# One GpSimd wait for two blocks' gather buffers in the edge loop of a graph network layer

## Chip, cores and metric

The kernel runs on one core of a Trainium2 chip (trn2). The metric is device time in microseconds; lower is better. Five engines run side by side and wait for one another through semaphores: PE (TensorE, matmuls), DVE (VectorE), ACT (ScalarE), POOL (GpSimd) and SP (SyncE, which here only issues DMAs).

## What is computed

One message-passing layer on 6250 nodes of 128 features and 100000 edges. Each edge gathers the rows of its two end nodes, a three-layer network makes a message, messages are averaged by destination, and a second network updates the node; a residual and a layer normalisation close it. Edges come sorted by destination (`col`).

```python
row, col = (edge_index[0], edge_index[1])
msg_in = jnp.concatenate([node_features[row], node_features[col]], axis=-1)
h = jax.nn.relu(msg_in @ Wm1 + bm1)
h = jax.nn.relu(h @ Wm2 + bm2)
messages = h @ Wm3 + bm3
agg = jax.ops.segment_sum(messages, col, num_segments=num_nodes)
...
agg = agg / jnp.clip(count, 1.0)[:, None]
node_in = jnp.concatenate([node_features, agg], axis=-1)
upd = jax.nn.relu(node_in @ Wn1 + bn1) @ Wn2 + bn2
return node_features + upd
```

## The kernel before

There are three stages. **Preparation** computes per node the two halves of the first product, x @ Wm1[:128] + bm1 and x @ Wm1[128:], and stores them in HBM as `a_table` (256 f32 a node) and `b_table`. **The edge loop** takes the edges in 391 blocks of 256 (EB; two halves of 128, TB = 2). **The node update** works on 49 windows of 128 nodes.

In the loop a block b goes through these steps, each on its engine and in that engine's program order; buffers rotate by the block's number:

- GpSimd (line 624) issues two indirect DMAs, one for each half: 128 rows of `a_table`, chosen by `src_idx`, into one of R = 4 buffer pairs of `a_edge`. Their landing counts on `s_g[b % 4]`. From the fifth block on it waits ahead of them (lines 621 and 622 of the source before) until PE has transposed block b - 4, whose buffers it fills: `s_ta` counts one for each block transposed.
- SP (lines 531 to 542) loads `rel` for two blocks at every even block, and, block by block, waits for both gathers of b (`s_g`, line 540) and issues the load of `b_win` (line 541), a window of 128 rows of `b_table`, into one of RB = 4 buffers. Once in four blocks it also reads the addresses of the next four windows from memory.
- DVE makes `onehot_t` of b (line 1013) when `b_win` of b has landed. In its program this stands two steps ahead: after the low part `h` (line 1104) of block b - 2.
- PE waits for `onehot_t` of b (`s_ot`), and this one wait covers the gathers too, since the `b_win` load was issued after their landing. It transposes the four 128x128 pieces of `a_edge` into PSUM (line 1365, four matmuls, the last counts on `s_ta`) and adds `b_win` x `onehot_t` (line 1311). Then it sums the messages of block b - 5 (lines 1328 to 1336, four matmuls) and does the second product of block b - 2 (line 1407, twelve matmuls), for which it waits for DVE's `h`.
- ACT takes relu of the first product (line 731), which DVE splits into a high and a low float32r part (line 1104), and likewise the second product (lines 721 and 1098). DVE also makes `onehot` (line 1028) and adds finished sums into `agg` (line 1050).

On SP, PE, ACT and DVE the blocks run in bodies of U = 4 in a hardware loop. GpSimd's loop over the blocks is unrolled: 387 waits and 782 gathers in a row, and no other work until the loop's end.

Of the kernel before, what the change touches and what calls it, by code (L numbers as in the profile page):

```python
# [19 lines left out]
R = 4  # L20
# [13 lines left out]
def gnn_layer(nc, x, src, dst, Wm1, bm1, Wm2, bm2, Wm3, bm3, Wn1, bn1, Wn2, bn2, out):  # L34
# [6 lines left out]
    NBE = -(-E // EB)  # L41
# [18 lines left out]
    with ExitStack() as ctx:  # L60
# [3 lines left out]
        def sem(name):  # L64
            return ctx.enter_context(nc.semaphore(name))
# [197 lines left out]
        s_ta = sem("s_a_transposed")  # L263
# [97 lines left out]
        def b_uses(k, g):  # L361

            return sum(b_at(j) == k for j in range(g))
# [202 lines left out]
        @block.gpsimd  # L566
        def _(pool):
            pool.memset(ident[:, :], 0.0).then_inc(s_zeros, 1)
            pool.wait_ge(s_zeros, 1)
            pool.affine_select(out=ident[:, :], in_=ident[:, :], compare_op=ALU.not_equal, fill=1.0,  # L570
                               base=0, pattern=[[-1, P]], channel_multiplier=1).then_inc(s_const, 1)
            pool.memset(edges_in[:, (GR - 1) * EB:GR * EB], PAD_DST).then_inc(s_pad, 1)
            pool.memset(edges_in[:, (2 * GR - 1) * EB:2 * GR * EB], 0).then_inc(s_pad, 1)
            pool.memset(f_x[:, NW - 1, :], 0.0).then_inc(s_xz, 1)
            pool.memset(ones2[:, :].bitcast(F32), 0.0).then_inc(s_zeros, 1)
            for rows in (b3_rows, bn2_rows):
                pool.memset(rows[:, :].bitcast(F32), 0.0).then_inc(s_zeros, 1)
            pool.wait_ge(s_zeros, 4)
            pool.memset(ones2[0:2, :].bitcast(F32), 1.0).then_inc(s_const, 1)
            pool.memset(h2_hi[:, :, :, H:HC].bitcast(F32), 1.0).then_inc(s_const, 1)  # L580
            pool.iota(node_half_i[:, :], pattern=[[P, NFE + 1]], base=0, channel_multiplier=1,
                      allow_small_or_imprecise_dtypes=True).then_inc(s_const, 1)
            pool.iota(first_node[:, :], pattern=[[P, NW]], base=0, channel_multiplier=0,
                      allow_small_or_imprecise_dtypes=True).then_inc(s_const, 1)
            pool.iota(iota16[:, :, :], pattern=[[0, TB], [1, P]], base=0, channel_multiplier=0,
                      allow_small_or_imprecise_dtypes=True).then_inc(s_const, 1)
            pool.memset(zeros[:, :], 0.0).then_inc(s_const, 1)
            pool.memset(from_quarter[:, :], 1.0).then_inc(s_mask, 1)
            pool.memset(to_quarter[:, :], 1.0).then_inc(s_mask, 1)
            pool.wait_ge(s_mask, 2)  # L590
            pool.affine_select(out=from_quarter[:, :], in_=from_quarter[:, :], compare_op=ALU.is_ge, fill=0.0,
                               base=0, pattern=[[-QUARTER, P // QUARTER]], channel_multiplier=1).then_inc(s_mask, 1)
            pool.affine_select(out=to_quarter[:, :], in_=to_quarter[:, :], compare_op=ALU.is_ge, fill=0.0,
                               base=-1, pattern=[[QUARTER, P // QUARTER]], channel_multiplier=-1).then_inc(s_mask, 1)
            pool.memset(words_act[0:1, :], 0).then_inc(s_wz, 1)
            pool.memset(words_pe[0:1, :], 0).then_inc(s_wz, 1)
            pool.memset(words_dve[0:1, :], 0).then_inc(s_wz, 1)
            pool.memset(row_step[0:1, :], 2).then_inc(s_wz, 1)
            pool.memset(row_far[0:1, :], 0).then_inc(s_const, 1)

            pool.wait_ge(s_edges, 16 * len(loads))
            pool.tensor_copy(edges_f[0:BG, GR:2 * GR, :],
                             edges_in[0:BG, GR * EB:2 * GR * EB].rearrange("p (g e) -> p g e", g=GR)
                             ).then_inc(s_efs, 1)
            dst_f = edges_f[0:BG, 0:GR, :]
            pool.tensor_copy(dst_f, edges_in[0:BG, 0:GR * EB].rearrange("p (g e) -> p g e", g=GR)).then_inc(s_efd, 1)

            pool.wait_ge(s_et, 2 * GR)
            pool.wait_ge(s_scr_rel, 16 * GR)
            pool.wait_ge(s_bz, 16)  # L610
            pool.wait_ge(s_w2s, 1)
            pool.wait_ge(s_fl, 1)
            pool.wait_ge(s_rw, 11)
            pool.memset(agg[:, :], 0.0).then_inc(s_zero, 1)

            for k in range(2):
                pool.wait_ge(s_as[k], 16 * ((NG + 1 - k) // 2))
            pool.wait_ge(s_bs[2], 16 * b_uses(2, NG))
            pool.wait_ge(s_ec, GR)
            for b in range(NBE):  # L620
                if b >= R:
                    pool.wait_ge(s_ta, b - R + 1)
                for t in range(TB):
                    pool.indirect_dma_start(a_edge[:, b % R * TB + t, :], None, a_table,  # L624
                                            bass.IndirectOffsetOnAxis(ap=src_idx[:, b * TB + t:b * TB + t + 1],
                                                                      axis=0)
                                            ).then_inc(s_g[b % R], 16)
            pool.wait_ge(s_w2, NBE)
            for k in range(2):
                pool.memset(f_row[k].bitcast(F32), 0.0).then_inc(s_frz, 1)  # L630
# [843 lines left out]
```

## Time and profile before

| | us |
|---|---|
| median of 3 timed runs | 1221.72 |
| the three runs | 1220.55, 1221.72, 1224.82 |
| span of the profiled execution | 1422.7 |
| edge loop in it, 89 to 1325 us | 1236 |
| PE busy / DVE / ACT / POOL in it, whole span | 1256.0 / 969.2 / 728.3 / 772.3 |

The profiled execution is a run of its own, and here it is 201 us longer than the timed median; recording weighs on this kernel. Times of records are true within it, and a timed run is shorter. PE's clock is granted in full (0.99 on average). A matmul's recorded end is modelled, and two neighbours overlap, so spacings of starts are read rather than lengths. A release that the profile can't name stands as "remote", and "issue" is idle time in which an engine waited for nothing that is shown.

### The profile page before, as it was taken

The page shows a single profiled execution, that of the slowest core. Times are in us where ns is not written, and L with a number is a line of the kernel's source. Part 1 is how long each engine was busy: PE and PEld are TensorE (multiplying, and loading weights), DVE is VectorE, ACT ScalarE, POOL GpSimd, SP SyncE. Part 2 cuts the span into 40 slices and gives each one's busy share as a digit, 9 for nine tenths or more (in the row PEclk, how much of TensorE's full clock was granted, in tenths as well). Part 3 has the DMA queues.
Part 4 walks back from the last instruction along what each step waited for, and adds up shares of the span by engine and source line. Part 5 has one row for each costly group of instructions (what it writes and reads, how often), then busy time and mean ns, then how long its engine had stood idle before and what let it go on. Part 6 is the DMA issues. An engine that isn't in the chain of part 4 may idle for free.

```text
span 1422.7 us, 34295 instructions
## 1 busy us (share of the span) xinstructions
PE 1256.0 (88%) x9586; PEld 1169.5 (82%) x9587; DVE 969.2 (68%) x2072; ACT 728.3 (51%) x1392; POOL 772.3 (54%) x814
## 2 busy tenths in 40 slices
PE   6978988888889988998889888999888988899897
PEld 5868888888888888888888888888888888888786
DVE  6856666666666666666666766767676776777676
ACT  3544554554554554554555454545545445455585
POOL 2166666666666665666666656666656666664000
PEclk9999999999999999999999999999999999999999
DMA  9765555455444545555445545454554445555012
GB/s 303 284 222 153 144 146 147 146 146 148 144 147 143 149 147 146 145 145 147 147 144 146 149 144 146 143 150 142 145 147 144 144 144 147 147 143 151 15 65 87
DMA packets 135603, 211.39 MB, mean 149 GB/s; under 512 B 24247, under 2 KB 102669, under 8 KB 134030
## 3 DMA queue, kind: packets, MB, share of 16 engines
q1 hardware_dynamic: 98030, 108.43, 25.5%
q0 software_dynamic: 37536, 102.55, 24.7%
q8 instruction: 13, 0.21, 0.1%
q14 instruction: 24, 0.20, 0.0%
HBM read 188.09 MB, written 22.80 MB: 148 GB/s over the span
## 4 chain that ended last, share of the span: by engine, by line
PE 58%; issue 16%; DVE 6%; another core or an unknown queue 6%; ACT 5%; DVEq 4%; DMA 2%; POOL 1%; SPq 1%; ACTq 0%
PE bank L1407 27%; PE bank L1365 9%; PE bank L1311 5%; PE sums L1328 4%; ACT bank L728 2%; PE sums L1332 2%; PE bank L1438 2%; PE sums L1336 2%; PE sums L1334 2%; ACT h L731 2%; PE sums L1451 1%; DVE h_lo L1098 1%; DVE onehot_t L1013 1%; DVE h L1104 1%
## 5 line engine op out<-in xcount | busy, mean ns | idle before, releaser
L624 POOL DMA_INDIRECT a_edge<-a_table,src_idx x782 | 752.9, 963 | 479.8 <-remote 280.5
L1407 PE MATMUL bank<-w,h 128*128 128x256 f32 x4692 | 655.4, 283 | 93.7 <-issue 92.6
L1407 PEld LDWEIGHTS bank<-w,h 128*128 128x128 f32 x4692 | 595.6, 189 | 116.7 <-issue 116.2
L721 ACT ACTIVATE h_hi<-bank 128x512 fp32r<-128x512 f32 x391 | 234.6, 600 | 453.3 <-remote 360.6
L1098 DVE SCALAR_TENSOR_TENSOR h_lo<-bank,h_hi 128x512 fp32r<-128x512 f32 x391 | 267.6, 685 | 137.5 <-issue 132.5
L1104 DVE SCALAR_TENSOR_TENSOR h<-bank,h 128x512 fp32r<-128x512 f32 x391 | 268.3, 686 | 105.9 <-ACT h L731 53.5
L731 ACT ACTIVATE h<-bank 128x512 fp32r<-128x512 f32 x391 | 234.1, 599 | 135.5 <-remote 62.2
L1365 PE MATMUL bank<-ident,a_edge 128*128 128x128 f32 x1564 | 241.8, 277 | 35.7 <-DVE onehot_t L1013 18.8
L1028 DVE SCALAR_TENSOR_TENSOR onehot<-iota,first_node,dst_col 128x256 fp32r<-128x256 int16 x391 | 187.4, 479 | 88.0 <-issue 86.5
L728 ACT COPY bank<-b_bc 128x512 f32<-128x512 f32 x391 | 234.8, 600 | 23.5 <-DVE h_lo L1098 17.4
L1365 PEld LDWEIGHTS bank<-ident,a_edge 128*128 128x128 f32 x1564 | 177.8, 141 | 54.2 <-DVE onehot_t L1013 30.7
L1311 PE MATMUL bank<-onehot_t,b_win 128*128 128x256 f32 x782 | 189.7, 324 | 0.9 <-issue 0.8
L1013 DVE TENSOR_SCALAR onehot_t<-rel,node_half 128x256 fp32r<-128x256 int16 x391 | 137.8, 352 | 11.9 <-DMA b_win<-b_table 9.3
L1328 PE MATMUL sums<-h_hi,onehot 128*128 128x258 f32 x391 | 125.3, 321 | 4.2 <-DVE h_lo L1098 1.0
L1311 PEld LDWEIGHTS bank<-onehot_t,b_win 128*128 128x128 f32 x782 | 119.1, 192 | 1.8 <-issue 1.6
L1332 PE MATMUL sums<-h_lo,onehot 128*128 128x256 f32 x391 | 114.5, 293 | 0.1
L1334 PE MATMUL sums<-h_hi,onehot 128*128 128x258 f32 x391 | 110.8, 283 | 0.0
L1336 PE MATMUL sums<-h_lo,onehot 128*128 128x256 f32 x391 | 109.7, 281 | 0.0
L1328 PEld LDWEIGHTS sums<-h_hi,onehot 128*128 128x128 f32 x391 | 73.4, 188 | 26.2 <-issue 22.2
L1332 PEld LDWEIGHTS sums<-h_lo,onehot 128*128 128x128 f32 x391 | 73.7, 188 | 5.3 <-issue 4.7
L1334 PEld LDWEIGHTS sums<-h_hi,onehot 128*128 128x128 f32 x391 | 74.5, 190 | 0.0
L1336 PEld LDWEIGHTS sums<-h_lo,onehot 128*128 128x128 f32 x391 | 73.7, 188 | 0.0
(186 smaller groups left out, 668.5 us busy)
## 6 DMA issues: line engine op xcount, KB each, us to landing
b_win<-b_table SPq DMA_DIRECT2D x391, 128.0 KB
rel<-rel_dram SPq DMA_DIRECT2D x196, 128.0 KB
a_edge<-a_table,src_idx POOLq DMA_INDIRECT x782
a_table<-work SPq DMA_DIRECT2D x12, 512.0 KB, 4.8
b_table<-work SPq DMA_DIRECT2D x5, 1024.0 KB
b_table<-h SPq DMA_DIRECT2D x4, 1024.0 KB
f_x<-in_x SPq DMA_DIRECT2D x12, 256.0 KB, 6.0
b_table<-a_edge SPq DMA_DIRECT2D x3, 1024.0 KB, 6.1
```

The lines of the kernel that those rows point to most:

```text
L624: pool.indirect_dma_start(a_edge[:, b % R * TB + t, :], None, a_table, bass.IndirectOffsetOnAxis(ap=src_idx[:, b * TB + t:b * TB + t + 1], ...
L721: act.activation(h2_hi[:, (k - AHEAD - 1) % U, :, 0:H], bank[H2[(k - AHEAD - 1) % U]][:, :].rearrange("p (t h) -> p t h", t=TB), ACT.Relu) ...
L728: act.copy(bank[H2[k % U]][:, :], b2_bc[:, :, :].rearrange("p t h -> p (t h)"))
L731: act.activation(h1[:, k % U, 0, :], bank[k % 2][:, :], ACT.Relu).then_inc(s_h1h, 1)
L1098: dve.scalar_tensor_tensor(h2_lo[:, j, :, :], bank[H2[j]][:, :].rearrange("p (t h) -> p t h", t=TB), 0.0, h2_hi[:, j, :, 0:H].bitcast(F32) ...
L1104: dve.scalar_tensor_tensor(h1[:, k % U, 1, :], bank[k % 2][:, :], 0.0, h1[:, k % U, 0, :].bitcast(F32), ALU.max, ALU.subtract).then_inc(s_ ...
L1311: ins = pe.matmul(bank[k % 2][:, h * EB:(h + 1) * EB], rows[:, h * P:(h + 1) * P], hot, start=False, stop=True, skip_group_check=True)
L1328: return pe.matmul(to[:, 0:HC], onehot[:, slot, 0, :], h2_hi[:, k % U, 0, :], start=start, stop=False, skip_group_check=True)
L1332: pe.matmul(to[:, 0:H], onehot[:, slot, 0, :], h2_lo[:, k % U, 0, :], start=False, stop=False, skip_group_check=True)
L1334: pe.matmul(to[:, 0:HC], onehot[:, slot, 1, :], h2_hi[:, k % U, 1, :], start=False, stop=False, skip_group_check=True)
L1365: ins = pe.matmul(bank[k % 2][:, h * EB + t * P:h * EB + (t + 1) * P], a_edge[:, k % R * TB + t, h * P:(h + 1) * P], ident[:, :], start=(t ...
L1407: ins = pe.matmul(to, h1[:, j, a, h * EB + t * P:h * EB + (t + 1) * P], w2[:, b, h, :], start=False, stop=(a == 1 and h == KH - 1), skip_g ...
```

## The change

```diff
@@ -618,8 +618,8 @@
             pool.wait_ge(s_ec, GR)
             for b in range(NBE):
-                if b >= R:
-                    pool.wait_ge(s_ta, b - R + 1)
+                if b >= R and b % 2 == 0:
+                    pool.wait_ge(s_ta, min(b - R + 2, NBE))
                 for t in range(TB):
                     pool.indirect_dma_start(a_edge[:, b % R * TB + t, :], None, a_table,
```

GpSimd waits at even blocks only, for both blocks whose buffers it fills next: ahead of the gathers of b and b + 1 it waits until b - 3 is transposed, where it waited for b - 4 ahead of b and for b - 3 ahead of b + 1. Four gathers follow each wait. Nothing else is altered; the buffers, the other engines' programs and the amount of work are the same.

GpSimd's instructions at the start of the edge loop, before. `a_edge` is the gather buffer, `a_table` the table in HBM, `s_a_transposed` the count of transposed blocks; the first eight gathers are those of blocks 0 to 3.

```order
L624 DMA a_edge<-a_table,src_idx 128x256 [waits s_b_stored2,s_edge_columns,s_a_stored1,s_a_stored0]
L624 DMA a_edge<-a_table,src_idx 128x256 x7
L624 DMA a_edge<-a_table,src_idx 128x256 [waits s_a_transposed]
L624 DMA a_edge<-a_table,src_idx 128x256
L624 DMA a_edge<-a_table,src_idx 128x256 [waits s_a_transposed]
L624 DMA a_edge<-a_table,src_idx 128x256
```

The same place on GpSimd with the change:

```order
L624 DMA a_edge<-a_table,src_idx 128x256 [waits s_b_stored2,s_edge_columns,s_a_stored1,s_a_stored0]
L624 DMA a_edge<-a_table,src_idx 128x256 x7
L624 DMA a_edge<-a_table,src_idx 128x256 [waits s_a_transposed]
L624 DMA a_edge<-a_table,src_idx 128x256 x3
L624 DMA a_edge<-a_table,src_idx 128x256 [waits s_a_transposed]
L624 DMA a_edge<-a_table,src_idx 128x256 x3
```

A wait now stands ahead of every fourth gather instead of every second; the gathers keep their order, and 194 waits remain of 387.

## Rows read from the trace of the kernel before

**Rows 1.** Busy time by stretch: start:end, length, each engine's busy us (instructions).
```profile
core 0: us, PE busy (x) PEld busy (x) DVE busy (x) ACT busy (x) POOL busy (x), PEclk, DMA share, GB/s
0.00:89.00 89.00, 67.19 (x446) 60.24 (x447) 63.60 (x115) 41.93 (x79) 24.59 (x37) 0.98 0.83 294
89.00:1325.00 1236.00, 1105.19 (x8601) 1036.06 (x8602) 839.98 (x1691) 624.24 (x1172) 747.70 (x778) 0.99 0.51 145
1325.00:1422.00 97.00, 83.64 (x541) 73.20 (x539) 65.64 (x266) 62.16 (x141) 0.00 (x0) 0.96 0.18 59
```

**Rows 2.** Costliest groups of the whole span: busy us, mean ns, idle before.
```profile
L624 POOL DMA_INDIRECT a_edge<-a_table,src_idx x782 | 752.9, 963 | 479.8 <-remote 280.5
L1407 PE MATMUL bank<-w,h 128*128 128x256 f32 x4692 | 655.4, 283 | 93.7 <-issue 92.6
...
L1013 DVE TENSOR_SCALAR onehot_t<-rel,node_half 128x256 fp32r<-128x256 int16 x391 | 137.8, 352 | 11.9 <-DMA b_win<-b_table 9.3
```

**Rows 3.** Chain of work that ended last: start us, length, what.
```profile
607.15 0.44 PE bank L1365 x4
...
609.73 0.44 PE bank L1365 x4
```

**Rows 4.** Instructions in time, 700 to 715 us: start, length, engine, line [idle before].
```profile
702.43 0.94 POOL L624 DMA_INDIRECT a_edge<-a_table,src_idx  x1 [0.30 <-issue]
...
703.62 0.34 DVE L1013 TENSOR_SCALAR onehot_t<-rel,node_half 128x256 fp32r<-128x256 int16 x1
...
704.02 0.65 PE L1365 MATMUL bank<-ident,a_edge 128*128 128x128 f32 x4
...
705.40 4.21 SPq L541 DMA_DIRECT2D b_win<-b_table  x2
...
707.55 0.94 POOL L624 DMA_INDIRECT a_edge<-a_table,src_idx  x1 [1.06 <-remote]
...
708.27 0.59 ACT L731 ACTIVATE h<-bank 128x512 fp32r<-128x512 f32 x1
...
708.80 0.95 POOL L624 DMA_INDIRECT a_edge<-a_table,src_idx  x1 [0.30 <-issue]
708.90 0.69 DVE L1104 SCALAR_TENSOR_TENSOR h<-bank,h 128x512 fp32r<-128x512 f32 x1 [0.32 <-ACT h L731]
...
709.50 0.36 DVE L1013 TENSOR_SCALAR onehot_t<-rel,node_half 128x256 fp32r<-128x256 int16 x1
...
709.92 0.66 PE L1365 MATMUL bank<-ident,a_edge 128*128 128x128 f32 x4 [0.19 <-DVE onehot_t L1013]
```

**Rows 5.** The same view at the loop's start; ACT L731 waits for PE L1311.
```profile
89.68 0.78 PE L1311 MATMUL bank<-onehot_t,b_win 128*128 128x256 f32 x2
...
90.49 0.60 ACT L731 ACTIVATE h<-bank 128x512 fp32r<-128x512 f32 x1 [2.56 <-issue]
...
93.23 0.78 PE L1311 MATMUL bank<-onehot_t,b_win 128*128 128x256 f32 x2
...
98.30 0.60 ACT L731 ACTIVATE h<-bank 128x512 fp32r<-128x512 f32 x1 [4.00 <-PE bank L1311]
```

**Rows 6.** The same view in three windows: DVE held by a late b_win load.
```profile
307.24 0.19 SPq L541 DMA_DIRECT2D b_win<-b_table  x1
...
309.87 0.35 DVE L1013 TENSOR_SCALAR onehot_t<-rel,node_half 128x256 fp32r<-128x256 int16 x1 [0.79 <-DMA b_win<-b_table]
...
774.27 1.17 POOL L624 DMA_INDIRECT a_edge<-a_table,src_idx  x1 [0.30 <-issue]
...
778.84 0.25 SPq L541 DMA_DIRECT2D b_win<-b_table  x1
...
781.53 0.35 DVE L1013 TENSOR_SCALAR onehot_t<-rel,node_half 128x256 fp32r<-128x256 int16 x1 [0.47 <-DMA b_win<-b_table]
```

**Rows 7.** Waits of the whole span: total us, times, longest.
```profile
DVE onehot_t L1013 <- DMA b_win<-b_table: 9.3, 18, 2.7
...
SPq L540 <- DMA a_edge<-a_table,src_idx: 166.7, 72, 3.6
```

## Prediction

> **What bounds the kernel now.** I read the table of stretches first: the edge loop takes 1236 us of the 1422.7 us span, 89 us of preparation stand ahead of it and 97 us of node update behind it, and PE is the busiest engine in the loop [rows 1]. The change touches only the loop, so only that stretch is worked out. The loop has 391 blocks (391 `onehot_t`, 782 gathers) [rows 2], so a block takes 1236 / 391 = 3.16 us in the profiled execution. The three timed runs have a median of 1221.72 us, 201 us below the profiled span. If the two ends keep their 186 us, the loop of a timed run is 1036 us, or **2.65 us a block**. In the chain of work that ended last, two neighbouring blocks of nothing but PE work begin their transposes at 607.15 and 609.73 us: 2.58 us apart [rows 3]. 391 x 2.58 is 1009 us, 97% of the timed loop: without the profiler PE is all but the whole bound, and it waits for hardly anything. The extra 0.5 us a block of the profiled execution is idle time called "issue" inside the matmuls of one line (92.6 us on PE) and on the other engines [rows 2].
>
> What releases PE? The transposes of block b wait for `onehot_t` of b (DVE), that one waits for the landing of `b_win` of b, SP issues this load only when both gathers of b have landed, and GpSimd issues the gathers only when the transposes of b - 4 have freed the buffers. So the gathers lie in a ring: **transposes, two gathers, b_win load, onehot_t, transposes**, four blocks round. The change lengthens this ring, and the question is whether it fits into PE's time.
>
> **The ring, link by link.** (a) Transposes to gathers. In the middle of the loop the transposes at 704.02 us are those of block 196 and the gather at 707.55 us is the first of block 200, freed by them: 3.53 us, although the transposes' records end at 704.67 and GpSimd had been idle for 1.06 us [rows 4]. ACT shows the same at the loop's start: at block 0 the activation starts at 90.49, 0.03 us after the recorded end of its matmuls (89.68 + 0.78); at block 2 these matmuls start at 93.23 and the activation at 98.30, after 4.00 us idle waiting for them [rows 5]. The distance is short at first and grows to a whole block within two blocks. I take most of it for the profiler's own burden on PE (it goes with the 201 us) and put 0.9 us for a timed run (0.65 for the transposes, and a reaction between 0.03 and a few tenths); 3.53 us stays as the upper bound. (b) Gather to gather is 1.25 us (707.55 to 708.80) [rows 4]. (c) Second gather to the `b_win` load: 702.43 to 705.40 is 2.97 us [rows 4], and 774.27 to 778.84 is 4.57 us [rows 6], where SP came late for other reasons. SP waited 72 times for a gather, 166.7 us in all [rows 7], so the landing often decides here; I take 3.4. (d) `b_win` load to `onehot_t`, where DVE waited for it: 778.84 to 781.53 is 2.69 us, 307.24 to 309.87 is 2.63 us [rows 6]; I take 2.65. (e) `onehot_t` to transposes: 703.62 to 704.02, 0.40 us [rows 4].
>
> Before: 0.9 + 1.25 + 3.4 + 2.65 + 0.4 = 8.6 us in four blocks, for which PE needs 4 x 2.65 = 10.6 us. There are 2.0 us to spare. In the profile DVE waited only 9.3 us in all for `b_win`, 18 times [rows 7], which agrees.
>
> **The change part by part.** It removes 193 of the 387 waits of GpSimd. Each wait costs GpSimd at most the 0.3 us of idle time that stands ahead of any gather anyway (707.55 + 0.94 to 708.80), and GpSimd is not at the end of the chain, so this gains nothing directly.
>
> What is left moves. *Even blocks*: the wait now asks for the transposes of b - 3, not b - 4. The gathers of b start one block later, and the ring of 8.6 us must close in three blocks, 3 x 2.65 = 7.95 us. It is 0.65 us too long. *Odd blocks*: the gathers of b + 1 wait for the same transposes as before, but now stand behind the two gathers of b that used to have gone ahead: 2 x 1.25 = 2.5 us more, a ring of 11.1 us in four blocks, for which PE needs 10.6. It is 0.5 us too long. Queued behind the one wait on GpSimd are thus four gathers; SP's `b_win` and `rel` loads, in order, wait for their landing, then DVE, then PE. Together: from an odd block's transposes, the even block three later starts at 8.6 us, the odd one behind it at the later of 11.1 and 8.6 + 2.58 = 11.2 us. Four blocks take 11.2 us, 2.80 a block, +0.15 on 2.65. **391 x 0.15 = 58 us, 1222 + 58 = 1280 us.** In the profiled execution, with link (a) at 3.53, the even ring is 11.2 us and four blocks take 11.2 + 2.58 = 13.8 us, 3.45 a block against 3.16: +113 us, a span near 1536 us.
>
> Bounds: with (c) at 2.97 the rings are 8.2 and 10.7 us and a block takes 2.69: +16 us. With (c) at 4.57 always they are 9.8 and 12.3, a block takes 3.09: +172 us. Link (a) can't be 3.53 us in a timed run: in the profile the way from the transposes of block 196 (704.02) over the activation (708.27), DVE's `h` (708.90) and `onehot_t` (709.50) to the transposes of block 198 (709.92) takes 5.90 us [rows 4], and a timed run does two blocks in 5.30, so at least 0.6 us of it is not there. With (a) at 2.9 a block takes (10.6 + 2.58) / 4 = 3.30: +254 us, the upper bound. Below nothing the change can only go by the rival named "faster".
>
> This link is the place where the Trainium skill bears on the case. The row shows 3.53 us from the transposes' start to the gather. The page "TensorE: Matmul & The Clock Gate", section "The cost: per-tile semaphore tail", gives the time from the last matmul's completion to its count as 25 ns plus a few ns a tile and 26 ns a count, under 0.1 us here; the page "Perfetto Trace Analysis", section "Per-instruction lifecycle: what the profiler-reported window actually captures", says that a matmul's end in the profile is estimated and its count comes outside the recorded window. By the first page link (a) would be about 0.75 us, an estimate, and the sum +43 us; by the row it would be the +254 us above. The trace's first block (0.03 us) agrees with the page, its third does not.
>
> **The rivals.** *It fits after all* (not slower): the links are shorter without the profiler. With (c) at 2.7 and (d) at 2.3 the rings are 7.55 and 10.05 us, below 7.95 and 10.6, and PE never waits: 1222 us, within 4 us. It decides from 7.95 us for the even ring on. For it: DVE is rarely held by `b_win` today [rows 7]. Against: today's slack of 2.0 us is what the change spends, 2.65 on even blocks and 2.5 on odd ones. *PE's counts are late in timed runs too*: with (a) between 1.6 and 2.9 us, (a + 7.7 + 2.58) / 4 is 2.97 to 3.30 a block, +125 to +254 us, 1347 to 1476 us. For it: the consumers really start that late, records or not [rows 4, 5]. Against: the timed run is 201 us shorter. *Faster*: with four gathers close together, the transfers of a pair overlap and SP issues two `b_win` loads with less between them, so that GpSimd's 2.5 us in each 2.65 us block lies in fewer, longer pieces and fewer of today's 27 us of leftover stalls (1036 - 1009) remain. It decides only if the rings fit; it could give back 5 to 15 us, 1210 us. Little speaks for it, since the leftover does not stand at gathers. *The change does not do what it says*: the order of instructions shows a wait ahead of every fourth gather, so I give this nothing. GpSimd itself as the limit also needs a look: four gathers take 5.0 us of the 5.3 us of two blocks, it is 6% from being one, and this makes every late wait hard to regain; at 1.33 us a gather it would be the bound.
>
> **How the numbers follow.** A loss of 4 to 125 us, forecast 1280 us: 0.50. Late counts, 1347 us and more: 0.24. It fits, within 0.3% (about what a measurement of this kernel can tell from no change): 0.20. Faster by more: 0.06. The range must leave out no more than 2 in 10: from 1220 us, which keeps the rival that it fits, to 1390 us, which takes in part of the late counts. Faster 0.06, same 0.20, slower 0.50 + 0.24 = 0.74.
>
> **What would show it.** After: GpSimd's gathers in groups of four, 1.25 us apart, with one idle time ahead of each group; more and longer waits of `onehot_t` for `b_win` (today 9.3 us in all; I expect over 60 us), and of the transposes for `onehot_t`; SP's waits for gathers well over today's 166.7 us; blocks in pairs, not evenly spaced; PE's busy time as before; preparation and node update unchanged at 89 and 97 us. Wrong would be the forecast if DVE's wait for `b_win` stays near 9 us, if the odd and even blocks are held alike, or if the profiled span grows much while the timed one does not: then link (a) is the profiler's, and the rest of the ring is shorter than I read it.

## The result and the profile after

| | before | changed |
|---|---|---|
| first comparison, median us | 1221.74 | 1364.47 |
| second, chip 15 (g1) | 1221.18 | 1368.1 |
| third, chip 13 (i1) | 1220.0 | 1362.93 |

The changed kernel is **11.7% slower** (ratio 1.117, 95% interval 1.113 to 1.121; 1.118 and 1.116 in the other two): 143 us, where 58 were forecast. The time lies in the stated range, near its upper end; the direction was right and the size wrong by a factor of nearly 2.5. Each ratio is of undisturbed runs, and one of g4's four runs further down, at 2866.2 us, is left out of it (the other three have a median of 1207.56 us).

One thing must be said of the times first. The kernel before has a median of 1220 to 1224 us on some chips (11, 13, 15 and the one of the first comparison, whose number is not on record) and of 1402 to 1404 us on two others (1 and 3), where no single run is below 1401 us. The profile ahead of the prediction, with its span of 1422.7 us, looks like the second kind: it has the same pauses and the same late counts. So its 201 us over the timed median are not the burden of recording, as was said ahead of the prediction: profiled and timed runs agree on either kind of chip (1223.9 us span in run j1, 1400.2 in run e0). What follows compares kernels on one chip, and j1 stands for the kernel before.

The stretches of the changed kernel, columns as in [rows 1], and then those of the kernel before in run j1 (PEld are PE's weight loads):

```profile
0.00:89.00 89.00, 66.81 (x452) 59.98 (x454) 63.62 (x116) 41.94 (x79) 25.88 (x38) 0.99 0.83 298
89.00:1265.00 1176.00, 1088.08 (x8598) 1021.67 (x8596) 833.53 (x1695) 649.51 (x1172) 747.09 (x777) 1.00 0.54 152
1265.00:1360.00 95.00, 83.34 (x538) 73.08 (x538) 64.24 (x262) 62.18 (x141) 0.00 (x0) 0.95 0.18 60
```

```profile
89.00:1129.00 1040.00, 1025.93 (x8607) 1012.84 (x8608) 825.71 (x1703) 643.06 (x1175) 758.03 (x779) 1.00 0.61 173
1129.00:1224.00 95.00, 83.82 (x534) 73.41 (x532) 62.82 (x256) 61.07 (x139) 0.00 (x0) 0.93 0.18 60
```

Preparation and node update are what they were, 89 and 95 us. The loop went from 1040 to 1176 us, and the weight loads of PE (second pair of numbers) do the same work in it, 1013 and 1022 us: PE waits. The waits name what for. The changed kernel, in total us, times, longest:

```profile
POOL a_edge L624 <- PE bank L1365: 233.2, 193, 3.3
DVE onehot_t L1013 <- DMA b_win<-b_table: 208.5, 182, 3.3
...
PEld bank L1365 <- DVE onehot_t L1013: 109.8, 138, 4.5
...
PEld sums L1328 <- issue: 37.2, 154, 1.2
```

The kernel before, run j1:

```profile
POOL a_edge L624 <- PE bank L1365: 120.3, 316, 2.2
...
DVE onehot_t L1013 <- DMA b_win<-b_table: 76.3, 114, 2.6
...
PEld bank L1365 <- DVE onehot_t L1013: 16.0, 19, 4.2
...
PEld sums L1328 <- issue: 8.2, 35, 1.2
```

GpSimd now waits 193 times, about once in two blocks. DVE waits 182 times for `b_win`, 133 times and 184 of the 208.5 us at even blocks (of which 194 are late), and in all 132 us more than before. PE's weight loads wait 94 us more for `onehot_t` and, a line that the forecast had not looked at, 29 us more for nothing that the profile shows ahead of the sums (L1328). These two make 123 of the loop's 136 us.

The ring can be followed in the trace of the changed kernel from 600 to 613 us: start, length, engine and line, and what ended the idle time before. SPq are the loads that SP issues.

```profile
600.54 0.60 PE L1365 MATMUL bank<-ident,a_edge 128*128 128x128 f32 x4
...
600.77 1.90 SPq L541 DMA_DIRECT2D b_win<-b_table  x2
...
601.41 0.94 POOL L624 DMA_INDIRECT a_edge<-a_table,src_idx  x1 [1.12 <-PE bank L1365]
...
602.66 0.94 POOL L624 DMA_INDIRECT a_edge<-a_table,src_idx  x1 [0.30 <-issue]
...
603.62 0.33 SPq L534 DMA_DIRECT2D rel<-rel_dram  x1
...
603.91 0.95 POOL L624 DMA_INDIRECT a_edge<-a_table,src_idx  x1 [0.30 <-issue]
...
605.16 0.95 POOL L624 DMA_INDIRECT a_edge<-a_table,src_idx  x1 [0.30 <-issue]
...
606.68 2.01 SPq L541 DMA_DIRECT2D b_win<-b_table  x2
...
608.97 0.47 DVE L1013 TENSOR_SCALAR onehot_t<-rel,node_half 128x256 fp32r<-128x256 int16 x1 [0.53 <-DMA b_win<-b_table]
...
609.50 0.66 PE L1365 MATMUL bank<-ident,a_edge 128*128 128x128 f32 x4 [0.51 <-DVE onehot_t L1013]
```

The transposes of odd block 173 (600.54) free GpSimd at 601.41, the second gather of block 176 starts at 602.66, SP loads its `b_win` at 606.68, DVE, which has been waiting, makes `onehot_t` at 608.97, and PE, which has been waiting too, transposes block 176 at 609.50: 0.87 + 1.25 + 4.02 + 2.29 + 0.53 = 8.96 us for three blocks. Averaged over the 183 even blocks from 20 to 384 the same five links are 0.89, 1.27, 3.62, 2.64 and 0.64 us, **9.05 us**. From an even block's transposes to the odd block's behind it there are 2.91 us. 9.05 + 2.91 = 11.96 us in four blocks is the 2.99 us a block of the whole loop. These are averages over all even blocks, not only those where every link was waited for: PE's weight loads waited for `onehot_t` 138 times, and where PE came later than `onehot_t` for another reason, link five is longer than the 0.4 us of a plain reaction.

### The profile page after: what moved, and what is told of

Same layout as the page of the kernel before. It is cut to its first block, busy times and chain, and to the rows that moved or that the text cites. A ratio compares the mean times of both kernels' runs of the same rounds, so it can differ in the third digit from the quotient of the medians.

```text
span 1359.8 us, 34295 instructions
## 1 busy us (share of the span) xinstructions
PE 1238.2 (91%) x9586; PEld 1154.7 (85%) x9587; DVE 961.4 (71%) x2072; ACT 753.6 (55%) x1392; POOL 773.0 (57%) x814
## 4 chain that ended last, share of the span: by engine, by line
DMA 36%; PE 34%; issue 10%; POOL 8%; DVE 6%; DVEq 4%; SPq 2%; ACT 0%
DMA a_edge<-a_table,src_idx 21%; DMA b_win<-b_table 14%; PE bank L1407 10%; POOL a_edge L624 8%; PE bank L1365 7%; DVE onehot_t L1013 3%; PE bank L1438 2%; PE sums L1328 2%; PE bank L1311 2%; PE sums L1451 1%; PE sums L1332 1%; PE bank L1221 1%; PE sums L1334 1%; PE bank L1423 1%; PE sums L1336 1%
## 5 line engine op out<-in xcount | busy, mean ns | idle before, releaser
L1407 PE MATMUL bank<-w,h 128*128 128x256 f32 x4692 | 618.0, 281 | 0.0
L1407 PEld LDWEIGHTS bank<-w,h 128*128 128x128 f32 x4692 | 582.0, 188 | 0.0
L728 ACT COPY bank<-b_bc 128x512 f32<-128x512 f32 x391 | 231.5, 592 | 252.3 <-DVE h_lo L1098 248.9
L1365 PE MATMUL bank<-ident,a_edge 128*128 128x128 f32 x1564 | 244.1, 279 | 81.9 <-DVE onehot_t L1013 80.9
L1013 DVE TENSOR_SCALAR onehot_t<-rel,node_half 128x256 fp32r<-128x256 int16 x391 | 143.2, 366 | 211.0 <-DMA b_win<-b_table 208.5
L1365 PEld LDWEIGHTS bank<-ident,a_edge 128*128 128x128 f32 x1564 | 174.2, 141 | 111.5 <-DVE onehot_t L1013 109.8
L731 ACT ACTIVATE h<-bank 128x512 fp32r<-128x512 f32 x391 | 232.4, 594 | 3.3 <-PE bank L1311 3.3
L1311 PE MATMUL bank<-onehot_t,b_win 128*128 128x256 f32 x782 | 189.0, 323 | 0.0
L1328 PE MATMUL sums<-h_hi,onehot 128*128 128x258 f32 x391 | 129.0, 330 | 7.3 <-DVE h_lo L1098 1.0
L1311 PEld LDWEIGHTS bank<-onehot_t,b_win 128*128 128x128 f32 x782 | 118.6, 192 | 0.2
L1334 PE MATMUL sums<-h_hi,onehot 128*128 128x258 f32 x391 | 110.3, 282 | 0.0
L1328 PEld LDWEIGHTS sums<-h_hi,onehot 128*128 128x128 f32 x391 | 73.2, 187 | 39.4 <-issue 37.2
```

The lines of the kernel that those rows point to most:

```text
L728: act.copy(bank[H2[k % U]][:, :], b2_bc[:, :, :].rearrange("p t h -> p (t h)"))
L731: act.activation(h1[:, k % U, 0, :], bank[k % 2][:, :], ACT.Relu).then_inc(s_h1h, 1)
L1311: ins = pe.matmul(bank[k % 2][:, h * EB:(h + 1) * EB], rows[:, h * P:(h + 1) * P], hot, start=False, stop=True, skip_group_check=True)
L1328: return pe.matmul(to[:, 0:HC], onehot[:, slot, 0, :], h2_hi[:, k % U, 0, :], start=start, stop=False, skip_group_check=True)
L1334: pe.matmul(to[:, 0:HC], onehot[:, slot, 1, :], h2_hi[:, k % U, 1, :], start=False, stop=False, skip_group_check=True)
L1365: ins = pe.matmul(bank[k % 2][:, h * EB + t * P:h * EB + (t + 1) * P], a_edge[:, k % R * TB + t, h * P:(h + 1) * P], ident[:, :], start=(t ...
```

## The experiments

All kernels below compute the full result.

**What sets the 2.99 us: the ring, the queueing, or a price for each late block.** Three kernels keep two gathers to a wait and move only which blocks wait for b - 3 instead of b - 4.

```diff
 # i2, every block
-                    pool.wait_ge(s_ta, b - R + 1)
+                    pool.wait_ge(s_ta, min(b - R + 2, NBE))
 # i3, one block in four (i4: b % 8)
-                    pool.wait_ge(s_ta, b - R + 1)
+                    pool.wait_ge(s_ta, b - R + (2 if b % 4 == 0 else 1))
```

> The changed kernel beside the kernel before and the three placements of the late wait, on one chip. Where the kernel before takes 1222 us: 1361 to 1373 us, as twice before. Where the kernel before takes about 1404 us: the ring bounds the changed kernel there too, and all blocks late took 1418 us there, so 1390 to 1430 us, within 2% of the kernel before, since there the late counts already cost what the ring costs here.

> Every block waits for b - 3 ahead of its own two gathers. Where the kernel before takes 1222 us: ring theory 1355 to 1375 us, queue theory 1222 us, count theory (0.73 us a late block) about 1500 us. Where it takes about 1404: 1418 us as twice before, and ring theory puts it within 20 us of the changed kernel.

> Only every fourth block waits for b - 3. Where the kernel before takes 1222 us: ring theory, 9.05 us and one PE step of 2.6 to 2.9 us in four blocks, 1325 to 1360 us; count theory 1293 us; queue theory 1222 us. Where it takes about 1404: 1471 us as twice before.

> Only every eighth block waits for b - 3. Where the kernel before takes 1222 us: ring theory, 9.05 us and five PE steps of 2.65 to 2.75 us in eight blocks, 1277 to 1300 us; count theory 1258 us; queue theory 1222 us. Where it takes about 1404: 1429 to 1434 us as twice before.

| on one chip, before 1220.0 us | late blocks | median us | ratio (95%) |
|---|---|---|---|
| changed kernel (i1) | 194 | 1362.93 | 1.116 (1.113 to 1.120) |
| all late (i2) | 387 | 1366.92 | 1.123 (1.118 to 1.128) |
| one in four (i3) | 97 | 1366.12 | 1.120 (1.117 to 1.123) |
| one in eight (i4) | 48 | 1309.65 | 1.073 (1.070 to 1.076) |

In i2 every block waits for its own release, and the loss is the same 147 us, so **the loss does not need an odd block queued behind an even one**. The run i3 can't say this: the gathers of block 4j + 1 ask for the same count as those of 4j, so they pass together, and in its trace they follow 1.28 us behind, one after another, as in the changed kernel. But i3 and i4 do rule out a price for each late block, since a quarter, a half or all of the blocks late cost the same 143 to 147 us, and an eighth costs 90. A ring of three blocks once in four sets the pace of all four. In the trace of i3 the way from the transposes of block 4j + 1 to those of 4j + 4 takes 8.88 us and the next step 3.12 us, 12.00 in four blocks; in i2 any three blocks take 9.0; in i4 the ring takes 8.70 us and the five steps behind it 3.22, 2.95, 2.72, 2.63 and 2.69, together 22.91 in eight, 2.86 a block. Two of the three missed what ring theory gave them: i3 lies 6 us above 1325 to 1360 us, i4 10 us above 1277 to 1300. The steps right behind the late block were put too low: 2.6 to 2.9 us in i3, where they take 3.12, and 2.65 to 2.75 in i4, where the first two take 3.22 and 2.95. The waits of i2 and then of i3 are nearly those of the change, with twice and half the late blocks:

```profile
DVE onehot_t L1013 <- DMA b_win<-b_table: 190.2, 182, 2.9
...
PEld bank L1365 <- DVE onehot_t L1013: 110.7, 130, 4.3
```

```profile
DVE onehot_t L1013 <- DMA b_win<-b_table: 224.8, 159, 4.4
...
PEld bank L1365 <- DVE onehot_t L1013: 113.4, 136, 4.8
```

**The same three on chips where the kernel before takes 1402 to 1404 us.**

> Every block waits for b - 3 instead of b - 4 ahead of its own two gathers; there are 387 waits and never four gathers behind one wait. Ring theory: each block is a three-block ring of about 9.05 us (0.89 + 1.27 + 3.62 + 2.64 + 0.64 in the changed kernel's trace), 3.0 a block, so about 1360 to 1370 us, as slow as the change. Queue theory (the loss comes from the odd block's gathers standing behind the even block's): 1222 us. Count theory (each late block costs 0.73 us, 143 us over 195): 387 late blocks, about 1500 us.

> Only every fourth block (b % 4 == 0) waits for b - 3; the others wait for b - 4 as in the kernel before. Ring theory: the slowest loop goes from block 4j + 1 over the ring of 9.05 us to block 4j + 4 and with one PE step of 2.6 to 2.9 us to 4j + 5: 11.65 to 11.95 in four blocks, 2.91 to 2.99 a block, 1325 to 1360 us, nearly the whole loss from half the late blocks. Count theory: 98 late blocks at 0.73 us, 1222 + 71 = 1293 us. Queue theory: 1222 us.

> Only every eighth block waits for b - 3. Ring theory: 9.05 us for three blocks and five PE steps of 2.65 to 2.75 us, 22.3 to 22.8 us in eight, 2.79 to 2.85 a block, 1277 to 1300 us. Count theory: 49 late blocks at 0.73 us, 1258 us. Queue theory: 1222 us.

They took 1418.73, 1472.95 and 1429.27 us beside 1404.05, and on a second such chip (h2, h3, h4) 1417.67, 1470.25 and 1434.41 beside 1402.48. Ring theory's numbers held in none of them, nor did the rivals'. That one late block in four is slower there (4.8 to 5.1%) than all late (1.0%) goes with one difference in the traces. The kernel before and the kernels with one late block in four or eight have, in these runs, 125 to 149 places inside the matmuls of L1407 where the next one starts over 0.3 us later, 91 to 101 us more than the usual spacing in all. With all blocks late (e1 and h2) there is none, and a released gather starts 1.3 us after the transposes. Why PE runs without these pauses when every block is late stays open. The changed kernel fell on no such chip, so what it does there wasn't measured.

**The pairs shifted by one.** The wait stands at odd blocks, for b and b + 1.

```diff
-                if b >= R and b % 2 == 0:
-                    pool.wait_ge(s_ta, min(b - R + 2, NBE))
+                if b == R or b > R and b % 2 == 1:
+                    pool.wait_ge(s_ta, min(b - R + (2 if b > R else 1), NBE))
```

> The changed kernel once more, beside the kernel before on the same chip. On the chip of the runs e0 to e3 the kernel before takes 1404 us, where it took 1222 us in the first comparison. If the change bounds the loop by its ring (9.05 and 2.9 us, 11.95 in four blocks), it does so on any chip: 1355 to 1375 us, faster than a kernel before of 1404 us and slower than one of 1222. If the difference of the chips adds to every kernel alike, it takes 1364 + 182, about 1546 us, there.

> The change with the pairs shifted by one: the wait stands at odd blocks, for b and b + 1, so that the late block is odd and the queued one even. Ring theory: as the changed kernel on the same chip, within 10 us. If SP's own work at even blocks (the rel load, and the addresses once in four blocks) is part of the ring, 10 to 30 us less than the changed kernel.

1356.55 us (ratio 1.111, 1.108 to 1.114) against 1368.1 us for the change on the same chip: 11.5 us less, at the lower edge of what was expected if SP's work at even blocks takes part. The records say where. From the second gather's start to its last data packet the late block takes about 3.15 us on average in g1 and 2.82 us in g2 (to the last landing count 3.5 and 3.2), and the whole ring 9.05 and 8.85. SP's `rel` load, issued at even blocks (at 603.62 us, between the `b_win` loads of 600.77 and 606.68 in the rows of the changed kernel), shares the DMA engines with an even block's gathers and not so much with an odd one's. It is an overlap that fits the numbers; it was not tested by itself.

**The `b_win` load out of the ring.** SP no longer waits for the gathers; DVE does, right ahead of `onehot_t`. The load of `b_win` then starts as soon as SP finds its buffer free, beside the gathers or ahead of them. At even blocks SP waits for that until PE has used `b_win` of b - 3 (it loads `rel` for two blocks there), and in g4 the load starts 1.55 us after the transposes of b - 3.

```diff
-                        if not isinstance(i, int) or i > 0:
-                            sp.wait_ge(s_g[k % R], nth(i, k, 16 * TB))
                         sp.dma_start(b_win[:, k % RB, :].bitcast(F32),
...
-                if isinstance(i, int) and U * i + k < U:
-                    dve.wait_ge(s_g[k % R], nth(i, k, 16 * TB))
+                dve.wait_ge(s_g[k % R], nth(i, k, 16 * TB))
```

It was made in the kernel before (g3), in the changed kernel (g4) and in "all late" (j2).

> The kernel before, with the wait for a block's gathers taken from SP, ahead of the b_win load, to DVE, ahead of onehot_t, so that the b_win load no longer lies in the ring. Ring theory: the ring has slack in the kernel before, so within 0.3% of it where it takes 1222 us. Where it takes 1404 us, the same unless the late counts of PE have used that slack up; then 10 to 60 us less.

> The changed kernel with the same move of the wait to DVE. Ring theory: the even ring is 0.9 + 1.25 + 2.9 (landing of the second gather) + 0.4 + 0.4 = 5.9 us in three blocks, for which PE takes 7.95, and the odd one 8.4 in 10.6: the change's whole loss goes and the time is that of the kernel before with the same move, within 5 us. Rival, four gathers in a row hold GpSimd or the DMA engines too long: it stays slower than that by 20 us or more. Rival, SP's loads are late and not the gathers: as the changed kernel.

> Every block waits for b - 3 (as in all_late), and the wait for the gathers stands on DVE, ahead of onehot_t, so that the b_win load is out of the ring. Ring theory: 0.9 + 1.25 + 2.9 + 0.4 + 0.4 = 5.9 us in three blocks against 7.9 for PE: 1200 to 1212 us, as g3 and g4. If holding a buffer pair one block longer costs by itself, 1300 us or more.

| | median us | before, same chip | ratio (95%) |
|---|---|---|---|
| before with the move (g3) | 1204.36 | 1221.18 | 0.985 (0.982 to 0.988) |
| changed with the move (g4) | 1208.35 | 1221.18 | 0.989 (0.986 to 0.992) |
| all late with the move (j2) | 1208.92 | 1223.66 | 0.987 (0.985 to 0.989) |

The whole loss goes, 1368 to 1208 us, with the single wait and the four gathers in a row still in place. So four gathers in a row cost by themselves at most the 4 us between g3 and g4, whose intervals overlap, and so do the buffers held a block longer (j2); the loss needs the serial load behind them. In g4 DVE waits for the gathers where it waited for `b_win`, and for less than half as long (in g3, g4 and j2 the lines of DVE and PE stand four higher, L1009 for L1013 and L1361 for L1365):

```profile
DVE onehot_t L1009 <- DMA a_edge<-a_table,src_idx: 78.9, 108, 1.8
...
PEld bank L1361 <- DVE onehot_t L1009: 7.9, 6, 4.8
```

g3 came out better than expected (within 0.3% of the kernel before): **it beats both kernels**, by 1.5% over the one before. So the kernel before was already losing some 17 us to this ring. Its 76.3 us of waiting for `b_win` in run j1 fit that, and in g3 that wait is 36.0 us:

```profile
DVE onehot_t L1009 <- DMA b_win<-b_table: 36.0, 81, 2.8
```

**The kernel before, profiled again.**

> The kernel before once more, for a second profile of it. If the late counts of PE in the first profile (3.2 us from the transposes of a block to the gather that they free, against 0.9 us in the profile of the changed kernel) belong to the recording of that one execution, a new profile shows about 0.9 us, a span near 1222 us, and blocks 2.65 us apart. If they belong to this kernel's execution, it shows 3.2 us again, with a span far from the timed 1222 us.

> The kernel before, for a profile on a chip where it takes 1222 us: blocks 2.65 us apart, gathers 0.9 us after the transposes' start where GpSimd waited for them, no pauses inside the matmuls of L1407, DVE waiting for b_win 20 to 60 us in all. Where it takes about 1404 us it repeats the first profile.

e0 (1402.0 us, span 1400.2) and h1 (1404.94 us) repeat the first profile but for its 20 us longer span: from a block's transposes to the gather that they free 3.07 us on average in e0, and pauses inside the twelve matmuls of L1407 (starts over 0.3 us apart), 143 of them, some 94 us in all. j1 (1225.63 us, span 1223.9) has none of these pauses, 0.92 us from transposes to gather, and blocks 2.63 us apart. DVE's wait for `b_win` was expected at 20 to 60 us and is 76.3. Two neighbouring blocks of j1, with the gather that the first one frees:

```profile
605.64 0.60 PE L1365 MATMUL bank<-ident,a_edge 128*128 128x128 f32 x4
...
606.76 0.98 POOL L624 DMA_INDIRECT a_edge<-a_table,src_idx  x1 [0.30 <-issue]
...
608.22 0.60 PE L1365 MATMUL bank<-ident,a_edge 128*128 128x128 f32 x4
```

In [rows 4] such a gather came 3.53 us behind the transposes. Here it is 1.12 us, and GpSimd was still busy with the gather ahead of it: 781.5 us busy in the span and, with 0.30 us between gathers, close to full in the loop.

## Why the prediction was right and wrong

- **What bounds the kernel, 2.65 us a block, 2.58 for PE alone.** Right: run j1 has 2.63 us a block and 89 + 1040 + 95 us, against the 1036 us of loop worked out from the timed median.
- **Link (a), 0.9 us instead of the trace's 3.53.** The value was right (0.92 before, 0.89 changed), and with it the choice against the rival "late counts". The reason given was wrong: the late counts and the 201 us do not come with being profiled. They come with the chip: the same kernel takes 1402 to 1406 us on two of them in all its timed runs, and 1224 with a profile on another. By that, the forecast of a profiled span near 1536 us failed; it was 1359.8.
- **The even ring as the cause.** Right, and shown by g4, where the loss goes with the `b_win` load out of the ring, and by i2, where it stays without the queue.
- **The odd ring, 11.1 us in four blocks.** It does not bind on average. In the changed kernel the last count of the odd block's `b_win` comes 0.70 us ahead of `onehot_t`, that of the even block's 0.24 us, and DVE waits for it 49 times, 25 us in all, at odd blocks. Taking 2.5 us of queueing for a second cause was harmless to the sum, since the even ring and the step behind it already came out longer.
- **The sum, 11.2 us in four blocks.** This is the step that failed: 11.96 were measured. Two terms of it are undersized. The ring is 9.05 us and not 8.6: link (c) 3.62 for 3.4, link (e) 0.64 for 0.40, the rest right to 0.02. And **the PE step behind the late block is 2.91 us and not 2.58**. (0.45 + 0.33) / 4 x 391 is 76 us; with 8 us because the kernel before has 2.63 and not 2.65 us a block, 58 becomes 142, the loss measured.
- **Why that step is longer.** 2.58 us was read where PE had just been busy [rows 3]. Behind a late block PE itself is slower; DVE, in order, also comes late, but seldom later than PE. In the trace of the changed kernel, a block that PE had not waited for, and then block 176, the late one:

```profile
606.26 0.60 PE L1365 MATMUL bank<-ident,a_edge 128*128 128x128 f32 x4
...
606.93 0.28 PE L1328 MATMUL sums<-h_hi,onehot 128*128 128x258 f32 x1
...
607.41 1.58 PE L1407 MATMUL bank<-w,h 128*128 128x256 f32 x12
```

```profile
609.59 0.48 DVE L1050 SCALAR_TENSOR_TENSOR agg<-sums,to_quarter,agg  x1
...
610.47 0.48 DVE L1028 SCALAR_TENSOR_TENSOR onehot<-iota,first_node,dst_col 128x256 fp32r<-128x256 int16 x1 [0.39 <-issue]
610.47 0.19 PEld L1328 LDWEIGHTS sums<-h_hi,onehot 128*128 128x128 f32 x1 [0.29 <-issue]
...
611.05 1.58 PE L1407 MATMUL bank<-w,h 128*128 128x256 f32 x12
...
611.47 0.68 DVE L1104 SCALAR_TENSOR_TENSOR h<-bank,h 128x512 fp32r<-128x512 f32 x1
612.07 0.34 DVE L1013 TENSOR_SCALAR onehot_t<-rel,node_half 128x256 fp32r<-128x256 int16 x1
...
612.47 0.66 PE L1365 MATMUL bank<-ident,a_edge 128*128 128x128 f32 x4
```

  From the transposes to the twelve matmuls of L1407 there are 1.15 us in the first (606.26 to 607.41) and 1.55 us in the second (609.50 to 611.05), with 0.29 us of "issue" ahead of the sums. It is so on average: between blocks 20 and 380 of the changed kernel this way takes 1.53 us in the 124 blocks for which PE had waited, and 1.15 us in g3, where it never waits. The twelve matmuls take the same time in both. The branches of the program lie on this way; that they are the reason was not tested. DVE comes from the late `onehot_t` (608.97) to the next one at 612.07, 3.10 us later, with its additions to `agg`, `onehot`, `h_lo` and `h` in between, and here it is ready just as PE is. In 98 of the 124 PE does not wait for the `onehot_t` of the next block, and its step is still 2.95 us; in the other 26 it does wait, and DVE's work is the later.
- **"GpSimd is not at the end of the chain; the waits saved gain nothing."** Right: with the ring out of the way, the kernel with one wait in two blocks (1208 us) is no faster than the one with a wait at each (1204 us).
- **The rival "it fits after all"** is refuted by 143 us, "faster" with it. The evidence cited for it, DVE's 9.3 us of waiting for `b_win` [rows 7], was read in an execution with slow blocks, which left the loads time; at 2.63 us a block it is 76.3 us. This was the warning that the slack of 2.0 us was already being used.

## What to carry to other kernels

A buffer's release is one link of a ring, and a wait that asks for one block more shortens that ring by a whole block, however few waits are saved: add up every link around it, each at its average and not its best, and compare with the number of blocks it spans times the block's time. One short ring in four blocks sets the pace for all four, and the steps right behind a stall are longer than the steady ones (2.9 to 3.2 us here for 2.6), so price them from a stretch that has stalls. Where the ring is too long, first take out the links that needn't be serial: a load that waits only to vouch for another transfer can start early, if the consumer waits for both.

## What the runs showed of the hardware

- One and the same kernel has medians of 1220 to 1224 us on at least three chips and 1402 to 1404 us on two others, steadily. On the latter PE's counts reach the other engines some 2 us later (3.07 against 0.92 us from transposes to gather), matmuls without any wait pause (94 us in all in e0), and PE's granted clock is no lower (0.99). The cause is open. The kernel with all blocks late has none of the pauses on these chips (e1, h2), and 1.3 us from transposes to gather.
- Indirect gathers on GpSimd start 1.25 us apart, two or four in a row, and their last data packet comes on average 2.8 us after their start in the changed kernel. Issuing them in groups of four made no difference beyond the 4 us between g3 and g4.
- A block's step on PE, with the same matmuls, takes 2.57 us where PE has not waited (g3), and 2.95 us behind a wait in the changed kernel, also where nothing that the profile shows holds it.
